# Edge counts from ten products a column instead of fifteen, and a slot table scattered over three blocks

## What is computed

```python
def _graph_encoder(x, edge_index, edge_type, W_rel, W_root, b_rgcn, W_gcn, b_gcn):
    seg = edge_type * n + dst
    agg = jax.ops.segment_sum(x[src], seg, num_segments=N_REL * n)
    cnt = jax.ops.segment_sum(ones, seg, num_segments=N_REL * n)
    mean = agg.reshape(N_REL, n, -1) / jnp.maximum(cnt, 1.0).reshape(N_REL, n, 1)
    h1 = jnp.einsum('rni,rio->no', mean, W_rel) + x @ W_root + b_rgcn
    ...
    out = jax.ops.segment_sum(xw[src] * norm[:, None], dst, num_segments=n)
```

## Time and profile before

| | |
|---|---|
| median of 3 runs | 1564.22 us (1563.77 to 1565.11) |
| profiled execution | 1566.67 us |
| its span, first to last instruction | 1564.3 us |
| TensorE busy | 1247.9 us (80%) |
| VectorE busy | 880.7 us (56%) |
| ScalarE busy | 725.3 us (46%) |
| GpSimd busy | 632.7 us (40%) |
| g1 begins | 160.72 us |
| a1 begins | 221.41 us |
| g2 begins | 372.94 us |
| a2 begins | 426.46 us |

### The profile page before, as it was taken

How to read it: one execution, slowest core, us unless ns; L and a number is a source line. 1 busy time by engine, 2 the same in 40 slices (tenths; PEclk the granted TensorE clock), 3 DMA queues, 4 the chain that set the end, 5 groups by cost and what they waited for, 6 DMA issues and landing times. The chain is left out here.

```text
span 1564.3 us, 32056 instructions
## 1 busy us (share of the span) xinstructions
PE 1247.9 (80%) x9846; PEld 938.1 (60%) x9847; DVE 880.7 (56%) x1703; ACT 725.3 (46%) x1089; POOL 632.7 (40%) x604
## 2 busy tenths in 40 slices
PE   8999584883866377846889999999999976863996
PEld 6777464783644365635666666666666644543775
DVE  8962667896566533325466666566666536664000
ACT  8994411874133253425354554456555434221554
POOL 0077746773500113322255555555555540011233
PEclk9998585895867579876999999999999996975899
DMA  3000200002034577747599999989999886735442
GB/s 129 1 1 4 82 17 1 1 1 73 18 91 119 180 248 206 209 97 295 180 247 273 271 287 273 275 237 299 285 276 285 243 232 181 210 84 177 86 98 52
DMA packets 116063, 247.39 MB, mean 158 GB/s; under 512 B 23588, under 2 KB 53537, under 8 KB 115990
## 3 DMA queue, kind: packets, MB, share of 16 engines
q1 hardware_dynamic: 80310, 162.88, 31.0%
q0 software_dynamic: 35680, 83.54, 23.8%
HBM read 215.14 MB, written 60.28 MB: 176 GB/s over the span
## 5 line engine op out<-in xcount | busy, mean ns | idle before, releaser
L627 PE MATMUL r_pO<-ring,r_rowsT 128*128 x2520 | 421.6, 326 | 0.0
L627 PEld LDWEIGHTS r_pO<-ring,r_rowsT 128*128 128x128 f16 x2520 | 243.9, 98 | 154.3 <-issue 0.7
L1837 DVE SCALAR_TENSOR_TENSOR ring<-q_wstage,ring 128x768 f16<-128x768 f32 x198 | 175.2, 953 | 58.8 <-ACT ring L1796 56.7
L1777 POOL DMA_INDIRECT acc_dram<-r_msg,r_scol x70 | 126.2, 1803 | 160.9 <-ACT r_msg L1825 77.0
L1796 ACT ACTIVATE ring<-q_wstage 128x768 f16<-128x768 f32 x198 | 148.8, 830 | 26.1 <-issue 26.1
L1825 ACT ACTIVATE r_msg<-r_pO,slot_inv 128x768 f32<-128x768 f32 x70 | 62.8, 896 | 190.8 <-PE r_pO L627 190.7
L477 POOL DMA_INDIRECT slot_inv<-qinv_dram,slot_pair x112 | 125.7, 1122 | 57.2 <-issue 33.5
L432 POOL DMA_INDIRECT slot_dram<-table_record,table_rowi x80 | 101.3, 1267 | 102.7 <-issue 102.1
L395 PE MATMUL acc<-oh_d,oh_s 125*125 125x512 f16 (+1 forms) x800 | 134.9, 308 | 0.0
L1898 PE MATMUL r_pT<-r_S,q_parts 128*128 128x128 f16 x852 | 101.0, 222 | 8.9 <-DVE r_S L1854 6.3
L1844 DVE TENSOR_TENSOR r_rowsT<-r_pT,r_rowsT 128x512 f16<-128x512 f32 x71 | 48.8, 688 | 98.9 <-ACT r_rowsT L1805 98.8
(11 more groups left out here) (398 smaller groups left out, 2416.3 us busy)
## 6 DMA issues: line engine op xcount, KB each, us to landing
q_wstage<-in_L_gnn_W_rel_dram SPq DMA_DIRECT2D x33, 2304.0 KB, 14.9
stage<-in_L_gnn_W_dram SPq DMA_DIRECT2D x6, 768.0 KB, 7.2
wparts<-in_L_ffn_w_dram SPq DMA_DIRECT2D x8, 576.0 KB
f_stage<-in_L_ffn_w_dram SPq DMA_DIRECT2D x8, 576.0 KB, 11.7
f_stage<-in_L_ffn_w_fast_dram SPq DMA_DIRECT2D x8, 576.0 KB, 6.1
f_stage<-in_L_ffn_w_slow_dram SPq DMA_DIRECT2D x8, 576.0 KB, 7.9
f_stage<-in_L_ffn_h_fast_dram SPq DMA_DIRECT2D x8, 576.0 KB, 9.1
down_dram<-f_stage SPq DMA_DIRECT2D x8, 576.0 KB
```

Of the source, the lines that this page charges most:

```text
L627: ins = eng.matmul(out, x, w[:, h * n:(h + 1) * n], start=first and x is xh and w is wh, stop=last and x is xl, **kw)
L1777: eng.indirect_dma_start(out=K.acc_dram[u % 2], out_offset=bass.IndirectOffsetOnAxis(ap=scol[:, u:u + 1], axis=0), in_=msg[:, u, :], in_of ...
L1837: ins_ = eng.scalar_tensor_tensor(wring[:, slot, 1, k, :], wstage[:, slot, k, :], W_SCALE, wring[:, slot, 0, k, :], ALU.mult, ALU.subtract)
```

## The change

Nothing but the first four blocks is touched; all later instructions are the same and in the same order.

1. The relation one-hot of a column (34 entries) is made by VectorE into the same buffer, behind the source one-hot, with an instruction of its own (80 in all). The products take `oh_d` as weights and the 659 columns of `oh_s` as what streams, in 512 and 147: ten a column. The sums are then rows by destination.
2. The first copies therefore fill `CT` (five of 512 by ScalarE, two of the rests by VectorE), mask and degree are made from them at once, and the transposes give `K.counts`.
3. The zeros of `empty` now lie in `c3`, so VectorE waits for the transfers that read them before it uses `c3`.
4. The scatters are split 40, 28 and 12 over the edge block, g1 and a1 instead of 46 and 34. The table is loaded in a1, after the 12. The gathers are split 72 and 40 instead of 80 and 32.

```diff
-TABLED_FIRST = 46
-INV_A1 = 80
+TABLED_EDGES, TABLED_G1 = 40, 68
+INV_A1 = 72
...
+            TAIL = REST + REL
...
-                        eng.tensor_scalar(oh_s[:, u, :], iota_n[:, :], srcf[:, j:j + 1], None, ALU.is_equal).then_inc(s["hots_s_ready"], 1)
+                        eng.tensor_scalar(oh_s[:, u, N:], iota_g[0:EP, :], etf[:, j:j + 1], None, ALU.is_equal)
+                        eng.tensor_scalar(oh_s[:, u, 0:N], iota_n[:, :], srcf[:, j:j + 1], None, ALU.is_equal).then_inc(s["hots_s_ready"], 1)
...
+                eng.wait_ge(s["emptied"], 16)
+                eng.wait_ge(s["sums_zeroed"], 32)
                 tg = c3[:, :].rearrange("p (t g) -> p t g", g=REL)
...
                 for i in range(NT):
-                    for piece in range(2 if i < NT - 1 else 1):
-                        a, cols = count_piece(i, piece)
-                        eng.copy(K.counts[:, i, cols], a).then_inc(s["counts_stored"], 1)
+                    eng.copy(CT[:, i, 0:512], acc[0:P, i, :]).then_inc(s["ct_stored"], 1)
...
                     for t in range(NT):
-                        tile = slice(t * P, (t + 1) * P)
-                        at = REST + t * REL
-                        eng.matmul(acc[0:P, 6, at:at + REL], oh_d[:, u, tile], onehot, start=False, stop=False, **kw)
                         for piece in range(2):
                             a, cols = count_piece(t, piece)
-                            last = eng.matmul(a, oh_s[:, u, tile], oh_d[:, u, cols], start=False, stop=False, **kw)
+                            last = eng.matmul(a, oh_d[:, u, t * P:(t + 1) * P], oh_s[:, u, cols], start=False, stop=False, **kw)
...
-                scatter_records(K, eng, s["tabled"], TABLED_FIRST, EJ)
+                scatter_records(K, eng, K.s_tabled, TABLED_EDGES, TABLED_G1)
...
+            if heads > 1:
+                eng.wait_ge(K.s_tabled, 16 * (EJ - TABLED_EDGES))
+                eng.dma_start(K.table["tables"][:, :, :, :].rearrange("t a l b -> t a (l b)"),
+                              K.slot_dram.rearrange("(a t l) b -> t a (l b)", a=2, l=128)).then_inc(s["table_loaded"], 16)
...
                 eng.sem_inc(s["out_free"], 2)
+                scatter_records(K, eng, K.s_tabled, TABLED_G1, EJ)
                 eng.wait_ge(s["columns_ready"], 1)
```

More of the change, by code:

```diff
@@ L333, in _ @@
                 eng.wait_ge(s["products_done"], 1)
[L334 to L337 removed]
+                for b, i0, n in ((5, 0, 3), (6, 3, 2)):
+                    tails = acc[0:P, b, 0:n * TAIL].rearrange("p (i r) -> p i r", r=TAIL)
+                    eng.tensor_copy(CT[0:P, i0:i0 + n, 512:N], tails[:, :, 0:REST]).then_inc(s["rest_stored"], 1)
+                    last = eng.tensor_scalar(qinv[:, i0:i0 + n, :], tails[:, :, REST:TAIL], 1.0, W_SCALE, ALU.max, ALU.mult)
+                link(last)
                 eng.reciprocal(qinv[:, :, :], qinv[:, :, :]).then_inc(s["qinv_ready"], 1)
+                eng.wait_ge(s["rest_stored"], 2)
                 for i in range(NT):
@@ L418, in _ @@
                         lo, hi = k * P, (k + 1) * P
-                        src = K.counts[:, k, i * P:(i + 1) * P]
+                        src = CT[:, k, i * P:(i + 1) * P]
                         if hi <= 512:
@@ L661, in gat_project @@
         W = Weights(K, name + "_w", rows_view(w), B["stage"], B["wparts"])
[L662 removed]
+        s = {n: K.sem(name + "_" + n) for n in ("a_loaded", "projected", "h_ready", "ones_ready", "inverse_gathered")}
         a_bc = B["a_bc"]
@@ L929, in spread_sources @@
                 spread(2 * b, B["cur"][:, b, 0, :]).then_inc(s["als_ready"], 1)
-            turns(eng, spread_sources, between=lambda: turn_tables(K, eng, K.s_table_loaded, psum[:, 6, 0:4 * T1]).then_inc(s["table_turned"], 1))
+            turns(eng, spread_sources, between=lambda: turn_tables(K, eng, s["table_loaded"], psum[:, 6, 0:4 * T1]).then_inc(s["table_turned"], 1))
             def multiply(h, b):
```

39 lines of the change are left out of this document (14 added, 25 removed).

## The result

The changed kernel takes **1579.99 us** (median of four runs, 1576.45 to 1583.48) where the kernel before takes 1563.99 beside it: a ratio of 1.011, interval 1.0086 to 1.0133. The forecast was 1576.2 in a range of 1568 to 1584, slower. The profiled execution took 1583.48, with a span of 1581.8; it is the slowest of the four, so its span is 17.5 us longer than before's, where the medians differ by 16.0.

What follows compares the result with a forecast made beforehand. TensorE bounds the edge block before the change, GpSimd after it. Edge block -8.6, first attention block +12.1 and second projection block +8.5 sum to +12.0 us on 1564.22, so 1576.2 us, range 1568 to 1584.

Steps and rivals of the forecast that it cites:

- edge block: First block: GpSimd's scatters become the bound, next block starts at 152.2 instead of 160.72, a gain of 8.6 us.
- g1: First projection block: 28 scatters instead of 34 and no table load gain nothing; cover for some ten scatters left unused.
- a1: First layer's attention block: twelve scatters delay the table load, VectorE reads at 245.4 instead of 233.27, +12.1 us.
- g2: Second projection block: 40 gathers instead of 32 set its end, next block at 435.0 against 426.46, +8.5 us.
- Products: Edge block, TensorE: ten products a column take 1.40 us instead of 1.690, ending at 132.4 against 144.24.
- The tail: End of the edge block, after the products: four short copies go, 12.1 us instead of 13.9.
- Rival A: Edge block: products get no cheaper, gain 1.9 instead of 8.6 us; +18.7, 1582.9 us in all; chance 0.08.
- VectorE's price: Edge block: each added 34-element instruction costs 0.10 us; 46 ahead of the slot ranks delay them 4.6 us.
- quiet step of 1.25: Second projection block: added gathers, mostly running when VectorE is finished, step at 1.25 us, making the term 7.0 instead of 8.5.
- Rival B: Edge block: clock falls in TensorE's pauses on VectorE, gain 4 instead of 8.6 us; +16.6, 1580.8; chance 0.09.
- C: Edge block's end through attention: clock stays up where now low, giving back 10.9 us; +1.1, 1565.3; chance 0.03.
- D: Attention and second projection: both waits are covered, only the edge block's gain remains; -8.6, 1555.6 us; chance 0.03.

Runs made afterwards that it cites:

- the kernel with the gathers moved: Kernel before with only the gathers re-split, 40 and 72 instead of 80 and 32; 1.0030 of the kernel before, fourth chip.
- split alone: Kernel before, fifteen products a column, with the change's splits: scatters 40, 28 and 12, gathers 72 and 40; 1.0071 of the kernel before, second chip.
- grouped kernel: Changed kernel, one relation one-hot instruction per up to four columns, scatters 40, 36, 4, gathers 80, 32; 0.9882 (third chip), 0.9898 (fourth) of the kernel before.

## Why the prediction was right in the whole, and where it was wrong

On the first chip the direction, the range and the two places of the loss came out as forecast; the sum up to a2 was +20.8 instead of +12.0. That the whole fell inside the range is partly luck: 20.8 on 1564.2 is 1585.0, just outside. From a2 on 3.3 us came off for a reason that no run places, and the profiled execution is the slowest of the four. The sizes that missed all missed to the same side: 4.6 us in the edge block, 1.9 in a1, 2.7 in g2. Step by step:

**Products, right.** 1.42 us a column against 1.40. Products end at 135.73 instead of 132.4: 2.3 of it because column 46 starts later (87.09 instead of 84.8), 1.0 because the 34 columns from there take 1.43 us each on average, (135.73 - 87.09) / 34. The tail is 12.06 us (137.44 to 149.50), forecast 12.1. TensorE's chain is done 6.4 us before the block ends, so GpSimd is the bound, as said. Rival A is out.

**VectorE's price, mis-sized.** I took 0.10 us from the 80-element row; an instruction of 34 elements with a scalar of its own for each partition costs 0.441 - 0.293 = 0.148 (seven pairs in 3.09). 46 of them are 6.8 us, and the first scatter moved by 6.71 instead of 4.6. The 40th scatter moved by more, to 153.05 from 144.10, 8.95: the other 2.2 are scatters that now meet VectorE at work. One takes 4.94 us and ends at 94.42, 1.1 after VectorE's comparison of 3808 elements (89.24 to 93.34). Before, a scatter met it later on and took 3.72, and it too ended 1.1 after (89.33, comparison 84.13 to 88.27), in the timeline of the kernel before:

```profile
84.13 4.14 DVE L306 TENSOR_TENSOR c<-iota_t,tin 128x3808 f32<-128x3808 f32 x1
...
85.61 3.72 POOL L432 DMA_INDIRECT slot_dram<-table_record,table_rowi  x1 [0.30 <-issue]
```

Others take 1.33 instead of 1.19. This is the rule of the Trainium skill that the prediction weighed for g2 (SBUF — State Buffer, "SBUF: two separate sides"), one block earlier than I looked for it: while VectorE holds the shared ports GpSimd cannot write descriptors. The trace agrees, as both scatters end behind the comparison at the same distance. The gain is 3.97 instead of 8.6, just outside its bounds (4.5 to 13.7). The step that failed here is the 0.10 us, a size read off a row of another kind, and the scatters' own delay, which had no term.

**g1, right,** 0.4 us. But the cover for ten more scatters was not there: eight more made it 3.0 us longer on the second chip (62.8 against 59.8) and 2.1 on the third (62.4 against 60.3).

**a1, right for the table, a piece missing behind it.** The read moved by 11.74 (forecast 12.1), with two errors against each other: the twelfth scatter is issued 17.25 us into the block instead of 16.5, and from the table load to the turn it is 2.57 instead of 3.8. What then made it 14.0 is the clock, which I had used only for the spreads. The last 50 products of the block, before:

```profile
349.40 7.34 PE L943 MATMUL a_ps<-h,parts 125*125 125x97 f32 x50 [3.43 <-DVE parts L834]
```

After:

```profile
356.39 9.98 PE L944 MATMUL a_ps<-h,parts 125*125 125x97 f32 x50 [3.43 <-DVE parts L834]
```

The windows around them, before:

```profile
348.00:354.00 6.00, 4.60 (x27) 4.61 (x28) 2.19 (x5) 0.50 (x1) 2.80 (x3) 0.72 0.02 0
354.00:360.00 6.00, 2.73 (x26) 2.57 (x24) 3.02 (x6) 0.45 (x1) 0.00 (x0) 0.99 0.00 1
```

And after:

```profile
355.00:361.00 6.00, 4.61 (x22) 4.61 (x23) 2.18 (x5) 0.49 (x1) 0.00 (x0) 0.51 0.01 3
361.00:367.00 6.00, 5.37 (x30) 5.20 (x29) 0.46 (x3) 0.00 (x0) 0.00 (x0) 0.64 0.00 0
```

After the same pause of 3.43 us the granted clock is 0.51 and then 0.64 instead of 0.72 and 0.99, and the group takes 2.64 us more. With -0.76 between the read and the first spread and +0.41 over the heads that is 11.74 + 2.64 - 0.76 + 0.41 = 14.0. Why the clock came back later in the one execution than in the other isn't shown.

**g2, right in kind, mis-sized.** 40 gathers bound it (11.2 instead of 8.5). The step is 57.0 / 39 = 1.462, forecast 1.438: 0.9 us. The rest is the end: I added a median landing of 4.4 and 0.84, 5.2 in all, and from the last issue to the next block it is 6.92. The landing was not the late part, the last gather landed 3.2 us after its issue, at 443.53. Behind it GpSimd still has an instruction at the block's end, a DRAIN, for which the sum had no term. It takes 3.31 us here (the three numbers are minimum, median and maximum in ns, then comes the start):

```profile
L656 POOLq DRAIN  x1: 3308/3308/3308, 443.7 to 443.7; - x1
```

And with 72 gathers in g2, in the kernel with the gathers moved:

```profile
L656 POOLq DRAIN  x1: 5922/5922/5922, 527.9 to 527.9; - x1
```

It is 3.31 in "split alone" as well, and 2.65 in the kernel before with its 32, where it was over at 425.0, before VectorE. So 3.2 + 3.3 + 0.4 stand where I had 4.4 + 0.84, and each gather adds 0.082 us to the end as well as its step. The quiet step of 1.25, which would have made this term 7.0, held for the last five gathers alone: three of the eight added ones still ran beside VectorE's work, and 7.0 would have been further off.

**Rival B** came true in its mechanism and cost nothing. Its figures were nearly met, a gain of 3.97 us against its 4 in the edge block and 1580.0 against its 1580.8 in all, but by coincidence: with B the products end at 141, and they ended at 135.73. TensorE's pauses on VectorE were there, 8.4 us in seven of them, the longest 2.11 us (44.88 to 47.00), and the clock fell once, after that one; two windows of the changed kernel:

```profile
40.00:50.00 10.00, 7.89 (x50) 5.63 (x49) 9.93 (x15) 10.00 (x15) 0.00 (x0) 0.89 0.01 2
50.00:60.00 10.00, 10.00 (x68) 6.97 (x67) 9.38 (x28) 10.00 (x15) 0.00 (x0) 0.93 0.00 0
```

It was back at 1.00 by 60 us, before column 46, and GpSimd was the bound anyway. On the fourth chip the same kernel had the same pause, 2.12 us, and its clock stayed at 1.00 in both windows, so such a pause does not bring it down every time. Taken strictly, as the prediction put it, the idle gaps would have made B the outcome; they did not. The grouped kernel kept 1.00 throughout this stretch. **C** did not happen: the granted clock was 0.50 from 149 to 157 us and 0.53 over the first 50 us of a1. **D** is out for a1 and g2 both, by the trace and by the kernels that undid the two waits.

**From a2 on** the span of the changed kernel is 3.3 us shorter with the same instructions. No experiment places this, and on the other chips the same instructions take 1128 to 1151 us.

On the fourth chip the sign was the other one, 0.9942. The prediction argued from one trace, and its terms had other sizes there: the edge block's gain 21.3 instead of 8.6, a1 -0.9 instead of +12.1, g2 +19.0 instead of +8.5. Nothing in that trace showed it.

## What to carry to other kernels

When a change makes one engine faster and puts the work on a second, look at what a third waits for: here VectorE's added 0.148 us a column, not TensorE's rate, set the time at which GpSimd could start, and so 6.4 of the 10.4 us that TensorE's chain had gained (159.88 to 149.50) were not collected. Give work to a later block only up to the point where its consumer in that block reads: four scatters were free in a1, twelve cost 12 us. Ask also what the giving engine still has to do behind its last transfer: here 0.082 us for each gather, for which the prediction had no term. And try an edit that is worth one per cent on more than one chip: the same pair of kernels was 1.1% slower on one and 0.3 to 0.6% faster on another.

## What the runs showed of the hardware

**A scalar per partition costs more than an operand.** VectorE's compare of 34 elements with a scalar of its own for each partition takes 0.148 us; the next instruction starts 0.15 after it (8.62 to 8.77). The same compare as an operation on two tensors, as the grouped kernel has it where a group is one column, takes 0.11 (23.24 to 23.35 us in the timeline of its second trace):

```profile
23.24 0.20 DVE L225 TENSOR_TENSOR oh_s<-iota_g,etf 125x34 f16<-125x34 f32 x1
23.35 0.38 DVE L227 TENSOR_SCALAR oh_s<-iota_n,srcf 125x625 f16<-125x625 f16 x1
```

**GpSimd's end of a block grows with its gathers.** The DRAIN behind the gathers of g2 takes 2.65 us with 32 of them, 3.31 with 40 and 5.92 with 72, the first two the same in every trace; in a1, where only gathers stand, it takes 3.32 with 40 and 6.58 with 80. That is 0.082 us for each. In a1 it is covered, because GpSimd is done long before the others; in g2 of the changed kernel on the first chip it is not. Where scatters stand in the block too the count is not so plain: 6.91 with 12 scatters and 72 gathers, but 6.58 with 12 and 80.

**Standing still beside indirect transfers.** On three of four chips the other engines nearly stopped while GpSimd issued gathers back to back every 1.25 us in a1, with the reason given as "issue" or "remote", and went on 12.2 to 13.7 us after the last one (in eleven of twelve traces; with 40 gathers it was 18.1, and the copy waited for TensorE). TensorE slowed down beside scatters in the edge block on two of them, in all three traces with fifteen products a column and hardly in those with ten. The pauses in a1 end with the transfers, and 40 gathers fewer made the block 44 us shorter, so the gathers are what they hang on; scatters alone were not varied for it. That it is the engines' instruction streams that arrive late fits the label "issue" and that fewer, longer instructions are spared; that is a guess, it was not measured, and why the first chip is free of it stays open.

**A pause before the 40th scatter.** GpSimd pauses before its 40th indirect transfer in all fourteen traces, for 2.40 to 2.43 us in thirteen of them and 3.29 in one, wherever in time that is. In "split alone":

```profile
146.00 1.20 POOL L432 DMA_INDIRECT slot_dram<-table_record,table_rowi  x1 [2.41 <-issue]
```

It is at 144.10 in the kernel before and at 153.05 in the changed one. With 39 scatters in the edge block it would fall into g1. That wasn't tried. The DRAIN at the end of that block is short, 0.13 us after 40 scatters and 0.63 after 46, six times 0.082 more. So it may be that the pause before the 40th clears up behind the first 39, as a DRAIN does; this is a guess from these two numbers.
